# Head attention: four 32-row score products beside each other on the array, and the loads, waits and roles that go with them

## The reference, cut to what matters

```python
x = x + attention(layernorm(x), weight)
def attention(x, weight):                    # x: (4, 1024, 128)
    y = x.reshape(4, 1024, 16, 8).transpose(0, 2, 1, 3)      # 16 heads of 8 features
    scores = einsum('bhtk,bhsk->bhts', y, y) / sqrt(8)
    attn = softmax(scores, axis=-1)
    o = einsum('bhts,bsc->bhtc', attn, x)    # every head weights all 128 features
    return o.transpose(0, 2, 1, 3).reshape(4, 1024, 16 * 128) @ weight
```

## Time and profile before

| what | value |
|---|---|
| median of 3 runs | 2970.72 us |
| the profiled execution: its time | 2974.2 us |
| the profiled execution: span from the first to the last instruction | 2972.4 us |
| heads, from the first score (675.0 us) to the end of the last addition to x (1709.0 us) | 1034 us |
| busy over the span: TensorE matmul, VectorE, ScalarE, GpSimd | 90%, 78%, 60%, 32% |
| mean granted TensorE clock | 0.932 of full |

### The profile page before, as it was taken

How to read it: one execution, slowest core, us unless ns; L and a number is a source line. 1 busy time by engine, 2 the same in 40 slices (tenths; PEclk the granted TensorE clock), 3 DMA queues, 4 the chain that set the end, 5 groups by cost and what they waited for, 6 DMA issues and landing times. The chain is left out here.

```text
span 2972.4 us, 35272 instructions
## 1 busy us (share of the span) xinstructions
PE 2665.9 (90%) x11635; PEld 2160.4 (73%) x11635; DVE 2309.3 (78%) x3342; ACT 1794.6 (60%) x2921; POOL 962.8 (32%) x761
## 2 busy tenths in 40 slices
PE   7899999979999999999999979999999883555688
PEld 5688888857888888888888757888888662444456
DVE  5777777848999999999999877778787547767555
ACT  3455555538888888888888734555555433444365
POOL 2567666640000000000000035666666303444300
PEclk8999999979999999999999989999999886777788
DMA  2566666631111111111111125666666000000000
GB/s 76 118 144 138 143 143 137 148 107 41 53 54 44 53 54 44 54 54 44 54 54 44 47 67 115 140 140 145 135 150 130 8 23 29 15 14 0 7 8 29
DMA packets 76838, 223.09 MB, mean 75 GB/s; under 512 B 12144, under 2 KB 16880, under 8 KB 76528
## 3 DMA queue, kind: packets, MB, share of 16 engines
q1 hardware_dynamic: 76432, 220.77, 30.1%
q10 hardware_dynamic: 224, 0.07, 0.0%
HBM read 205.87 MB, written 10.75 MB: 73 GB/s over the span
## 5 line engine op out<-in xcount | busy, mean ns | idle before, releaser
L613 POOL TENSOR_TENSOR moe_experts_lo<-moe_experts_hidden,moe_experts_hi 128x512 fp32r<-128x512 f32 x512 | 660.8, 1291 | 341.4 <-ACT moe_experts_hi L551 341.3
L870 DVE TENSOR_TENSOR heads_e_lo<-heads_e,heads_e_hi 128x1024 fp32r<-128x1024 f32 x512 | 624.3, 1220 | 75.2 <-ACT heads_e_hi L819 66.2
L814 ACT ACTIVATE heads_e<-psum 128x1024 f32<-128x1024 f32 x512 | 524.3, 1024 | 131.9 <-PE psum L763 131.8
L558 ACT ACTIVATE psum<-psum 128x512 f32<-128x512 f32 x512 | 298.0, 582 | 479.8 <-PE psum L90 479.8
L585 DVE TENSOR_TENSOR moe_experts_weighted<-moe_spread,psum 128x512 f32<-128x512 f32 x512 | 351.1, 686 | 190.4 <-PE psum L90 186.6
L88 PE MATMUL psum<-moe_n_hi,moe_w_lo 128*128 128x512 f32 x1024 | 400.7, 391 | 4.8 <-PEq L54 4.5
L88 PE MATMUL psum<-heads_e_hi,heads_v_lo 128*128 128x512 f32 x1024 | 400.5, 391 | 0.7 <-DVE heads_u L838 0.7
L89 PE MATMUL psum<-moe_n_lo,moe_w_hi 128*128 128x512 f32 x1024 | 400.1, 391 | 0.0
L90 PE MATMUL psum<-moe_n_hi,moe_w_hi 128*128 128x512 f32 x1024 | 400.0, 391 | 0.0
L90 PE MATMUL psum<-heads_e_hi,heads_v_hi 128*128 128x512 f32 x1024 | 399.6, 390 | 0.0
L89 PE MATMUL psum<-heads_e_lo,heads_v_hi 128*128 128x512 f32 x1024 | 399.1, 390 | 0.0
(11 more groups left out here) (426 smaller groups left out, 4529.1 us busy)
## 6 DMA issues: line engine op xcount, KB each, us to landing
moe_spread<-moe_mask SPq DMA_DIRECT2D x128, 1024.0 KB, 9.9
heads_scale<-heads_inverse_copy SPq DMA_DIRECT2D x64, 512.0 KB, 3.8
heads_left<-heads_parts SPq DMA_DIRECT2D x128, 64.0 KB
heads_right<-heads_parts SPq DMA_DIRECT2D x128, 64.0 KB
moe_experts_raw<-in_gate SPq DMA_DIRECT2D x16, 256.0 KB
moe_experts_raw<-in_up SPq DMA_DIRECT2D x16, 256.0 KB, 11.6
moe_experts_raw<-in_down SPq DMA_DIRECT2D x16, 256.0 KB, 11.6
heads_parts<-heads_e_hi SPq DMA_DIRECT2D x16, 256.0 KB, 3.0
```

What stands on the lines that cost most here:

```text
L558: act.activation(psum[:, GATE + p % 2, :], psum[:, GATE + p % 2, :], ACT.Silu).then_inc(silu_ready, 1)
L613: pool.tensor_tensor(lo[:, p, :], hidden[:, p % 2, :], f(hi[:, p, :]), ALU.subtract).then_inc(low_ready, 1)
L814: act.activation(e[:, s % 4, :], wide, ACT.Exp, scale=HEAD ** -0.5, accum_out=sums[:, h % 2, s:s + 1]).then_inc(exp_done, 1)
L870: dve.tensor_tensor(e_lo[:, s, :], e[:, s % 4, :], f(e_hi[:, s, :]), ALU.subtract).then_inc(low, 1)
```

## The change

Left and right now hold the head's 32 rows four times, at partitions 0, 32, 64 and 96. Two tiles of scores are issued together as four matmuls of 32 rows, each reading another 32 partitions and writing another bank. They wait until both exponentials of the pair before are done. Each head therefore has 8 loads of 64 KB for right and 8 for left. Those for right are issued by SyncE, now behind the spread of the inverses; those for left by GpSimd, as soon as the scores of the head two before are done. The tiles whose high part ScalarE makes are 1, 3, 5 and 7, the trail is 6 tiles, TensorE's loop goes in steps of two tiles, and scale_sums stays behind tile 5. The clearing of left and right is gone. The layernorm no longer waits for its copies; the first loads of a batch wait for that batch's six copies, and the first four high parts do as well, since they overwrite the source of a copy.

```diff
@@ layernorm
-                            sp.dma_start(to[:, chunk(c)], f((n_hi, n_lo)[part][:, chunk(c)])).then_inc(copied, 16)
-                    sp.wait_ge(copied, 16 * len(copies) * CHUNKS)
+                            sp.dma_start(to[:, chunk(c)], f((n_hi, n_lo)[part][:, chunk(c)])).then_inc(copied[c // HALVES], 16)
@@ head_attention
+        copied = [sem(f"copied{b}") for b in range(BATCH)]
+        BATCH_COPIED = 16 * 3 * HALVES
-        HEAD_LOADS = 4
-        ACT_HIGH = (0, 2, 4, 6)
-        TRAIL = 7
+        HEAD_LOADS = 8
+        ACT_HIGH = (1, 3, 5, 7)
+        TRAIL = 6
+        def load_head(eng, tile, orders, h, loaded):
+            at = slice(h // HEADS * T, (h // HEADS + 1) * T)
+            dims = slice(h % HEADS * HEAD, (h % HEADS + 1) * HEAD)
+            if h % HEADS == 0:
+                eng.wait_ge(copied[h // HEADS], BATCH_COPIED)
+            for i, order in enumerate(orders):
+                for g in range(4):
+                    row = 32 * g + i * 2 * HEAD
+                    eng.dma_start(f(tile[row:row + 2 * HEAD, h % 2, :]),
+                                  parts_dram[dims, order:order + 2, at]).then_inc(loaded[h % 2], 16)
@@ sync
-                sp.wait_ge(zeroed, 2)
-                load_head(0)
-                load_head(1)
+                load_head(sp, right, (0, 1), 0, right_loaded)
+                load_head(sp, right, (0, 1), 1, right_loaded)
                 for h in range(COUNT):
                     sp.wait_ge(inverse_ready, h + 1)
...
-                    if h + 2 < COUNT:
-                        sp.wait_ge(scores_done, (h + 1) * TILES)
-                        load_head(h + 2)
                     sp.wait_ge(inverse_stored, 16 * (P // 32) * (h + 1))
                     after(sp, scaled_ready, (h - 1) * HALVES)
                     sp.dma_start(scale[:, h % 2, :], inverse_dram[h % 2:h % 2 + 1, :].to_broadcast([P, T])
                                  ).then_inc(scale_loaded[h % 2], 16)
+                    if h + 2 < COUNT:
+                        sp.wait_ge(scores_done, (h + 1) * TILES)
+                        load_head(sp, right, (0, 1), h + 2, right_loaded)
+            @block.gpsimd
+            def _(pool):
+                load_head(pool, left, (0, 0), 0, left_loaded)
+                load_head(pool, left, (0, 0), 1, left_loaded)
+                for h in range(2, COUNT):
+                    pool.wait_ge(scores_done, (h - 1) * TILES)
+                    load_head(pool, left, (0, 0), h, left_loaded)
@@ tensor
-                    after(pe, exp_done, h * TILES + s - 1)
-                    for half in range(HALVES):
-                        last = pe.matmul(psum[:, SCORES + 2 * (s % 2) + half, :], left[:, h % 2, s * P:(s + 1) * P],
-                                         right[:, h % 2, half * BANK:(half + 1) * BANK], start=True, stop=True)
-                    last.then_inc(scores_done, 1)
+                    after(pe, exp_done, h * TILES + s)
+                    for tile in (s, s + 1):
+                        for half in range(HALVES):
+                            g = 2 * (tile % 2) + half
+                            rows = slice(32 * g, 32 * (g + 1))
+                            last = pe.matmul(psum[:, SCORES + g, :], left[rows, h % 2, tile * P:(tile + 1) * P],
+                                             right[rows, h % 2, half * BANK:(half + 1) * BANK], start=True, stop=True)
+                        last.then_inc(scores_done, 1)
...
-                for n in range(COUNT * TILES + TRAIL):
+                for n in range(0, COUNT * TILES + TRAIL, 2):
                     if n < COUNT * TILES:
                         scores(n // TILES, n % TILES)
-                    if n % TILES == TRAIL and n // TILES >= 2:
-                        add_head(n // TILES - 2)
                     if n >= TRAIL:
-                        weighted_rows((n - TRAIL) // TILES, (n - TRAIL) % TILES)
+                        if n % TILES == TRAIL and n // TILES >= 2:
+                            add_head(n // TILES - 2)
+                        for m in (n - TRAIL, n - TRAIL + 1):
+                            weighted_rows(m // TILES, m % TILES)
@@ scalar, and the same in vector
+                        if n < BATCH:
+                            act.wait_ge(copied[n], BATCH_COPIED)
@@ vector
-                    if s == TRAIL - 2 and h >= 1:
+                    if s == TRAIL - 1 and h >= 1:
                         scale_sums(h - 1)
@@ gpsimd
-                pool.memset(f(right[:, :, :]), 0.0).then_inc(zeroed, 1)
-                pool.memset(f(left[:, :, :]), 0.0).then_inc(zeroed, 1)
```

More of the change, by code:

```diff
@@ L131, in layernorm @@
 def layernorm(nc, tag, psum, consts, x, n_hi, n_lo, affine=None, keep=None,
-              splits=(), loads=(), copies=None, x_dram=None):
+              splits=(), loads=(), copies=None, copied=None, x_dram=None):
     inv, eps, identity, row_pick = consts["inv"], consts["eps"], consts["identity"], consts["row_pick"]
@@ L164, in layernorm @@
         tiles_loaded, split_high, split_low = sem("tiles_loaded"), sem("split_high"), sem("split_low")
-        copied, x_loaded = sem("copied"), [sem(f"x_loaded{c}") for c in range(CHUNKS if x_dram is not None else 0)]
+        x_loaded = [sem(f"x_loaded{c}") for c in range(CHUNKS if x_dram is not None else 0)]
         def chunk(c):
@@ L675, in head_attention @@
         inverse_dram = nc.dram_tensor(f"{tag}_inverse_copy", (2, T), F32, kind="Internal").ap()
+        copied = [sem(f"copied{b}") for b in range(BATCH)]
+        BATCH_COPIED = 16 * 3 * HALVES
         layernorm(nc, f"{tag}_norm", psum, consts, x, row_hi, row_lo,
-                  splits=[(dram["head_w"], w_hi[:, :], w_lo[:, :])], copies=[(parts_dram[:, 0, :], 0), (parts_dram[:, 1, :], 1), (parts_dram[:, 2, :], 0)])
+                  splits=[(dram["head_w"], w_hi[:, :], w_lo[:, :])], copies=[(parts_dram[:, 0, :], 0), (parts_dram[:, 1, :], 1), (parts_dram[:, 2, :], 0)],
+                  copied=copied)
         left = sb(f"{tag}_left", [P, 2, T], F32R)
@@ L689, in head_attention @@
         SCORES, OUT, SUM = 0, 4, 6
-        zeroed, heads_loaded = sem("zeroed"), [sem("heads_even"), sem("heads_odd")]
+        left_loaded, right_loaded = ([sem(f"{side}_{parity}") for parity in ("even", "odd")] for side in ("left", "right"))
         turned, v_by_act, v_by_dve = sem("turned"), sem("v_by_act"), sem("v_by_dve")
@@ L759, in scores @@
                     if s == 0:
-                        pe.wait_ge(heads_loaded[h % 2], 16 * HEAD_LOADS * (h // 2 + 1))
-                    after(pe, exp_done, h * TILES + s - 1)
-                    for half in range(HALVES):
-                        last = pe.matmul(psum[:, SCORES + 2 * (s % 2) + half, :], left[:, h % 2, s * P:(s + 1) * P],
-                                         right[:, h % 2, half * BANK:(half + 1) * BANK], start=True, stop=True)
-                    last.then_inc(scores_done, 1)
+                        pe.wait_ge(left_loaded[h % 2], 16 * HEAD_LOADS * (h // 2 + 1))
+                        pe.wait_ge(right_loaded[h % 2], 16 * HEAD_LOADS * (h // 2 + 1))
+                    after(pe, exp_done, h * TILES + s)
[6 more added lines that the diff above has]
+                        last.then_inc(scores_done, 1)
                 def weighted_rows(h, s):
@@ L867, in _ @@
                         after(dve, out_done, n - (TILES - 1))
+                        if n < BATCH:
+                            dve.wait_ge(copied[n], BATCH_COPIED)
                         dve.tensor_copy(e_hi[:, s, :], e[:, s % 4, :]).then_inc(dve_high, 1)
@@ L881, in _ @@
                 dve.wait_ge(added, BATCH * HALVES)
-            @block.gpsimd
-            def _(pool):
-                pool.memset(f(right[:, :, :]), 0.0).then_inc(zeroed, 1)
-                pool.memset(f(left[:, :, :]), 0.0).then_inc(zeroed, 1)
 def recurrent_layer(nc, tag, psum, consts, dram, x, out=None):
```

## The result

The changed kernel takes 2940.28 us (median of 4 runs, 2938.73 to 2943.87) against 2970.58 for the kernel before: ratio 0.9901, 95% interval 0.9884 to 0.9918. That is 30.3 us faster where 63 were forecast. The sign and the range held; the size was twice too large.

The account below looks back on a forecast made before the run. TensorE was taken to bound the kernel, with VectorE close behind; 15.95 - 14.95 - 0.05 = 0.95 us per head over 63 heads is 60, plus tail 1 and start 2: -63, so 2907.5 us, range 2898 to 2962.

Parts of the forecast that it names:

- The bound before: In the kernel before, TensorE's seventy matmuls per head at 0.2278 us make 15.95 us, the whole period.
- The group: Four score matmuls side by side on TensorE: 0.23 us of streams plus 0.32 for two drains, 0.55.
- R1: Group dearer than 0.62 us, TensorE stays the bound; at 0.75, -30 us, 2941; chance 0.22 with light R3 or R4.
- The wait at the turn: Where a head begins, TensorE can stand 1 us for PSUM that scale_sums frees; charged 0.05 us per head.
- the clock was no rival: TensorE kept the full clock in the last stretch and would be busy 13.3 to 14.5 of 14.95 us afterwards.
- VectorE's floor: VectorE's work per head is unchanged, so about 14.95 us per head is the floor whatever TensorE gains.
- The covers: ScalarE's copy hides the group; SyncE's order and GpSimd's queue fit their loads within the head; each costed at nothing.
- The start: Without the wait for copies, the heads' block begins 2.3 us earlier; gain 2, range from 2.3 to -7.
- R3: VectorE's high parts and GpSimd's loads shut each other out: up to +90 us, 3060; slow-side cases together 0.16.
- R4: GpSimd's queue sets the period from 1.87 us per load: -22 us at 1.95, +53 at 2.1; slow-side cases together 0.16.
- The 3.07 times: Skill's gain for four row tiles of 512 columns, by which a group would be estimated at 0.30 us.

Follow-up runs that it names:

- fastest version: Changed kernel with VectorE multiplying by the spread inverses ahead of the low part of tile 5: 2909.79 us, ratio to the kernel before 0.9796.
- a further group in the same mode: Changed kernel with each group of four issued twice in a row into the same banks, only the second signalled: 2981.85 us.

## Why the prediction was right and wrong

**The bound before** was read rightly: in turn, with all else of the change in place, the time is that of the kernel before.

**The group, the step that failed first.** The form of the term was right, a stream plus two edges. Its size was not: 0.23 + 0.32 = 0.55 was written and 0.69 measured, as the edges cost 0.46. The prediction priced an edge by what a matmul's record runs beyond the next start, 0.16. The trace shows more than that in the edges: the weight load, which elsewhere hides under the matmul before, is not pulled across. That this load is the cause, and not the array running empty, isn't shown. TensorE's head is then 12.30 + 2.76 = 15.06, above VectorE's 14.95. This is rival R1 in kind, which had 0.22 with its neighbours; its threshold was written as 0.62 and is (14.95 - 12.30) / 4 = 0.66 by the same numbers. The measured 2940.28 is close to the 2941 worked out there for a group of 0.75, though by a dearer wait on a cheaper group; that agreement is luck.

**The wait at the turn, the step that failed second.** Its place, its mechanism and its length ahead of any shrinking (up to 1 us) stood in the prediction, and it was charged at 0.05 on the ground that TensorE had 0.45 us of room. With a group of 0.69 TensorE has none: it measured 0.39 (nearly eight times the charge), and taking it away gave 30.5 us. Per head: 15.06 + 0.39 = 15.45, against the measured 15.46. The gap of 0.46 to the 15.00 of the forecast (14.95 + 0.05) is 0.11 for the group beyond VectorE's floor and 0.34 for the wait. Over 63 heads that is 29 us of the 33 missing; the heads behind the three additions to x, 0.8 each, are 2 more. The profiled execution lost some 3 us more in its first three heads at the lower clock. The prediction said that the clock was no rival and looked at a stretch at the end only; that held for all heads but these.

**VectorE's floor** of 14.95 was not reached by the changed kernel. The fastest version's heads are at 15.02 and, for thirteen heads behind the late one, at 14.96 (1382.71 to 1577.18 us), where VectorE is busy for 69.20 of 70.00 us and TensorE for all 70.00 (1430 to 1500). So the floor of 14.95 was met there and not passed, but with both engines full it wasn't tested by itself.

**The covers held.** ScalarE's copy between the second exponential and the group (undone: +104), the order on SyncE (undone: +80), GpSimd as the second queue (undone: +118). Each was costed at nothing with the work that hides it, and each costs more than the whole gain when that cover is gone. The start: the block begins 2.3 us earlier relative to the copies' issue, as worked out, and the first score keeps 1.4 of it where 2 were forecast.

**R3 and R4 didn't happen.** GpSimd's load takes 0.56 us where 1.0 was taken and 1.87 would have set the period, and the high parts take 690 ns beside it, at most 697. What there is of R3 is on the other engine: one load in eight takes 1.01 us beside a high part, in a queue that has room for it.

**The Trainium skill's rules.** The measured edges, 0.46 us per group at 32 rows and at 64, fit what the Trainium skill has in TensorEngine Tiling, section Tiling Modes, that changing the mode drains the array; the rows show the price, not the draining itself. The 3.07 times of the Trainium skill's TensorE: Matmul & The Clock Gate, section Part 3, does not carry over: a group embedded in 128-row work gains 0.91 / 0.69 = 1.3, while a further group in the same mode costs 0.23, about four times less than in turn. The Trainium skill's rule in SBUF — State Buffer, section Who interferes with whom, that a VectorE copy in its two-port mode and GpSimd's making of descriptors exclude each other, fits the load of 1.01 us beside a high part. That the first to start keeps the ports doesn't fit as it stands: this load began at 1011.30, ahead of the high part at 1011.53, and was still the one that took longer.

## What to carry to other kernels

Row tiles between full matmuls pay per change of mode, not per matmul: count the edges, 0.46 us here for the way in and the way out together, and put more small matmuls into one group where PSUM has banks for them (not tried here; the further group above went into the same banks). When a change moves two engines to within 1% of each other, price waits between them at their full length, since there is no slack left to absorb them, and look for the one instruction whose place in a queue decides the wait: moving one multiplication ahead of one subtraction doubled the gain. Work that was costed at nothing should be listed with its cover, because here each of the three that were undone was worth more than the change.

## What was not expected of the hardware

GpSimd issues a load of 16 rows by 4 KB in 0.56 us (median of 512), less than SyncE's 0.65, with a landing 2.5 us after. VectorE's high part beside it takes as long as without it (690 and 694 ns), while the load takes 1.01 us and not 0.55. Weight loads at the edges of a group of row tiles start together with their matmuls, with 0.36 us in which none runs on the way in and 0.24 on the way out, and the matmuls there keep the same distances for 64 rows as for 32.
